# One row buffer instead of two for the second expert layer of a two-layer decoder kernel

## What is computed

```python
pos = jnp.sum(jnp.cumsum(oh, axis=0) * oh, axis=-1) - 1      # place of a token in its expert
valid = pos < CAP                                             # CAP = 192
xb = jnp.zeros((E, CAP + 1, H), x.dtype).at[flat_e, pos_c].set(x[tok])   # E = 48 experts
gu = jnp.einsum('ech,eoh->eco', xb, gate_up_proj)
g, u = jnp.split(gu, 2, axis=-1)
out = jnp.einsum('eci,ehi->ech', silu(g) * u, down_proj)
final = jnp.zeros_like(x).at[tok].add(y * w[:, None])         # 8 experts of a token summed
...
x = layernorm(x + final)
```

## Time and profile before

| | us |
|---|---|
| median of 3 runs | 2174.53 |
| lowest, highest run | 2170.31, 2190.89 |
| span of the profiled execution | 2197.3 |
| of it, first to last even scatter issue in `kept_experts` | 1798.09 to 2151.90 |
| of it, first load issue of `finish` to the end | 2158.30 to 2197.3 |

### The profile page before, as it was taken

The page is one execution under the profiler, slowest core; times in us unless marked ns, Lnnn a source line. Parts: engine busy times, 40 slices in busy tenths (PEclk is TensorE's granted clock), DMA queues, the critical chain, the costliest instruction groups (busy, mean ns, idle before and its releaser), DMA issues. The chain is left out here.

```text
span 2197.3 us, 34584 instructions
## 1 busy us (share of the span) xinstructions
PE 1743.9 (79%) x9155; PEld 1385.2 (63%) x9156; DVE 1522.4 (69%) x2887; ACT 959.1 (44%) x1867; POOL 1110.5 (51%) x806
## 2 busy tenths in 40 slices
PE   4899889247999999999999798687841159999990
PEld 4566565126888888888888455464521158888880
DVE  5466776664777787777887323978879657777774
ACT  4355362221444444434444323535333147777773
POOL 1000624553677777777687200025447647777761
PEclk9898999666999999999999898888875579999995
DMA  6011011024777787888887511021010269999867
GB/s 262 1 39 58 20 58 39 1 78 150 202 201 191 197 233 201 209 211 216 205 244 163 189 44 38 23 74 58 1 58 1 91 205 260 258 254 255 255 156 251
DMA packets 134248, 310.14 MB, mean 141 GB/s; under 512 B 30632, under 2 KB 31240, under 8 KB 132520
## 3 DMA queue, kind: packets, MB, share of 16 engines
q1 hardware_dynamic: 68728, 196.24, 25.7%
q0 software_dynamic: 63168, 108.89, 24.6%
q10 hardware_dynamic: 2288, 4.29, 0.5%
HBM read 234.48 MB, written 93.16 MB: 149 GB/s over the span
## 5 line engine op out<-in xcount | busy, mean ns | idle before, releaser
L98 POOL DMA_INDIRECT tab_rows<-pair,slot x256 | 312.6, 1221 | 487.0 <-DVEq L751 314.6
L1253 POOL DMA_INDIRECT xg<-x_rows,ids x167 | 211.3, 1265 | 65.6 <-issue 42.6
L90 PE MATMUL gu<-wgu_h,xgT_h 128*128 x648 | 234.5, 362 | 6.9 <-DVE xgT_l L1429 4.1
L90 PE MATMUL gu<-wgu_l,xgT_h 128*128 x648 | 220.2, 340 | 0.0
L90 PE MATMUL gu<-wgu_h,xgT_l 128*128 x648 | 219.1, 338 | 0.0
L1262 POOL DMA_INDIRECT odd_rows<-ysb,ids x80 | 149.0, 1862 | 76.0 <-DMA odd_rows<-ysb,ids 41.5
L1262 POOL DMA_INDIRECT acc_rows<-ysb,ids x80 | 141.6, 1769 | 67.6 <-DMA acc_rows<-ysb,ids 33.1
L1309 ACT ACTIVATE ysb<-yp,wts 128x512 f32<-128x512 f32 x160 | 110.2, 688 | 144.0 <-PE yp L1536 112.3
L90 PE MATMUL guk<-xgT_hk,wgu_hk 128*128 128x192 f32 x576 | 161.2, 280 | 0.0
L1429 DVE TENSOR_TENSOR xgT_l<-tpx,xgT_h 128x512 fp32r<-128x512 f32 x163 | 112.3, 689 | 68.5 <-ACT xgT_h L1295 62.9
L1299 ACT ACTIVATE sg<-gu 128x192 f32<-128x192 f32 x162 | 53.6, 331 | 240.2 <-PE gu L90 214.8
(11 more groups left out here) (498 smaller groups left out, 5067.8 us busy)
## 6 DMA issues: line engine op xcount, KB each, us to landing
wgu_sb<-in_wgu SPq DMA_DIRECT2D x64, 768.0 KB
wgu_sbk<-in_wgu SPq DMA_DIRECT2D x48, 768.0 KB
wd_sb<-in_wd SPq DMA_DIRECT2D x64, 256.0 KB
wd_sbk<-in_wd SPq DMA_DIRECT2D x48, 256.0 KB
ct<-in_ctxT SPq DMA_DIRECT2D x8, 1024.0 KB
wd_sb<-in_wd SPq DMA_DIRECT2D x64, 128.0 KB
wd_sbk<-in_wd SPq DMA_DIRECT2D x48, 128.0 KB
odd_rows<-zero SPq DMA_DIRECT2D x1, 4352.0 KB, 15.3
```

The lines of the kernel that those rows point to most:

```text
L90: i = nc.tensor.matmul(out, left(k), right(k), start=(start and k == 0 and m == 0), stop=(k == ops - 1 and m == 2))
L98: nc.gpsimd.indirect_dma_start(out=tab, out_offset=bass.IndirectOffsetOnAxis(ap=s["slot"][:, n:n + 1].bitcast(U32), axis=0), in_=s["pair"] ...
L1253: nc.gpsimd.indirect_dma_start(out=xg[:, t % G, :], out_offset=None, in_=x, in_offset=bass.IndirectOffsetOnAxis(ap=ids[:, t:t + 1].bitcast ...
```

## The change

Both tiles of an expert are now added into `acc1`. Tile t with t of 2 or more waits for both tiles of the preceding expert. For an even tile, those are t-2 and t-1. For an odd tile, they are t-3 and t-2, for which the even tile ahead of it has already waited. `odd1` is gone, and so are its clear in `mixer_two` and its eight loads and sixteen adds in `finish`. The counts of the semaphores follow. The order of the instructions on each engine is unchanged.

```diff
 def kept_experts(nc, d, s):
 
-    tab, x, acc = d["tab1"], d["x5"], (d["acc1"], d["odd1"])
+    tab, x, acc = d["tab1"], d["x5"], d["acc1"]
...
             def scatter_add(t):
                 if t >= 2:
-                    pool.wait_ge(s_add[t % 2], (t // 2) * 16)
+                    for n in range(2):
+                        pool.wait_ge(s_add[n], (t // 2) * 16)
                 pool.wait_ge(s_ye, t + 3)
                 nc.gpsimd.indirect_dma_start(
-                    out=acc[t % 2], out_offset=bass.IndirectOffsetOnAxis(ap=ids[0:rows(t), t:t + 1].bitcast(U32), axis=0),
+                    out=acc, out_offset=bass.IndirectOffsetOnAxis(ap=ids[0:rows(t), t:t + 1].bitcast(U32), axis=0),
...
             for n in ("x5", "acc1"):
                 sp.dma_start(d[n][TOK:TOK + P, :], zero[:, :]).then_inc(s_zero, 16)
-            clear_rows(sp, d["odd1"], zero, s_zero)
...
-            sp.wait_ge(s_zero, 128)
+            sp.wait_ge(s_zero, 112)
...
-        BASE, FIRST, LATER = B * 20, 3 * GT, 2
+        BASE, FIRST, LATER = B * 20, 2 * GT, 2
...
             for n in range(NG):
-                for t, dst in ((d["acc1"], xb), (d["odd1"], xbo)):
-                    sp.dma_start(dst[:, n, :, :], rows(t, n)).then_inc(loaded[n][0], 16)
+                sp.dma_start(xb[:, n, :, :], rows(d["acc1"], n)).then_inc(loaded[n][0], 16)
...
             for n in range(NG):
                 sem_n, there = loaded[n]
-                dve.wait_ge(sem_n, there + 32)
-                for j in range(GT):
-                    c.done(nc.vector.tensor_tensor(xb[:, n, j, :], xb[:, n, j, :], xbo[:, n, j, :], ALU.add))
-                c.wait()
+                dve.wait_ge(sem_n, there + 16)
```

More of the change, by code:

```diff
@@ L2071, in _ @@
                 settle(pool, passed)
-                pool.wait_ge(s_zero, 128)
+                pool.wait_ge(s_zero, 112)
                 scatter(nc, d["tab1"], s, E1 * REG1 - 1, s_scat)
@@ L2220, in step @@
                 if b is None:
-                    act.wait_ge(s_zero, 128)
+                    act.wait_ge(s_zero, 112)
                 averaged(a)
@@ L2767, in finish @@
         xb = sb("xb5", [P, NG, GT, D])
-        xbo = sb("xbo5", [P, NG, GT, D])
         xo = sb("xo5", [P, NG, GT, D])
@@ L2778, in finish @@
         loaded = [(s["mixer"][0], 2 * B * 16 + 16), (s["mixer"][1], 2 * B * 16), (s["weights"][0], NI * 16), (s["weights"][1], NW * 16),
-                  (s["mixer"][7], 128), (s["router"][0], 2 * ROUTED), (s["router"][1], 2 * ROUTED), (s["router"][4], 2 * ROUTED)]
+                  (s["mixer"][7], 112), (s["router"][0], 2 * ROUTED), (s["router"][1], 2 * ROUTED), (s["router"][4], 2 * ROUTED)]
         passed = s["passed"]
@@ L2911, in build @@
     for n, rows, cols, dt in (("x2", TOK + P, D, F32), ("x5", TOK + P, D, F32), ("acc0", TOK + P, D, F32), ("acc1", TOK + P, D, F32),
-                              ("odd0", TOK + P, D, F32), ("odd1", TOK + P, D, F32),
+                              ("odd0", TOK + P, D, F32),
                               ("tab0", E0 * REG0 + P, 2, I32), ("tab1", E1 * REG1 + P, 2, I32)):
```

## The result

| | before | changed |
|---|---|---|
| median of 4 runs, us | 2178.56 | 2236.54 |
| lowest to highest run | 2170.31 to 2190.89 | 2224.46 to 2241.88 |
| span of the profiled execution | 2197.3 | 2222.7 |

The ratio is 1.0251 with a 95% interval of 1.021 to 1.0292: the changed kernel is 2.5% slower, about 55 us. The forecast was +26.4 us, 1.2%, with a range up to 2224. The direction was right. The size was half of what came, and the median lies outside the range.

A forecast was written before the change was run, and what follows sets the result against it. ACT, DVE and PE were taken to pace the kernel, with POOL's closed chain taking over after the change. +36.1 + 1.7 - 11.4 = +26.4 us on the median gave 2200.9 us, 1.2% slower, range 2182 to 2224.

The forecast's parts named there:

- What bounds the kernel: Steady part of the second experts: ACT, DVE and PE set the pace, 7.67 us an expert; add into HBM hidden.
- The closed chain: POOL, second experts: even issue, gather, odd issue, odd landing, wake-up, next even issue; period 8.51 us, +36.1 us.
- sign of being wrong: Wrong if the steady period stays under 8.1 us or passes 9 us, or last stage returns under 8 us.
- L: POOL's time from odd scatter start to the start its landing permits: 5.3 us; above 4.45 us experts pay.
- the bound by packets: POOL's queue q0 in the kernel before: odd scatter landed 3.8 to 4.7 us after start, so L 4.7 to 5.6 us.
- The fixed phase: POOL against DVE: ACT and DVE follow the odd landing, phase much like today's, so the 2.22 us odd issue stays.
- collides with the expert weights: Rival, second experts: odd tile shares engines with weights; period 10.2 us, time 2282, about 2235 at half; chance 0.08.
- The last experts: Last four intervals, without gathers: each takes 6.40 us, 25.6 us against 23.94, +1.7 us.
- Who is behind the wait: Gathers queued behind POOL's wait run ten tiles ahead; ACT stops for `ysbk` first, so PE's transposes do not starve.
- The last stage: Half the loads and 16 DVE adds go; ACT paces groups at 2.24 us; -11.4 us, bounds 8 to 13.
- The clear: Clear of 4352 KB, 14.8 us: nobody listed as waiting for POOL's loads behind it, counted as 0.
- The clock: Rival: granted clock falls as PE idles; at 0.87 no cost, at 0.75 +52 us more; chance 0.03.

The follow-up runs named there:

- buffer_by_expert: Kernel before with both tiles of an expert in one buffer, the next expert's in the other, waits two experts back: 0.9972 times before.
- the two wait experiments: Kernel before, each scatter waiting for both preceding-expert tiles: 1.0284 times before. Changed kernel, odd scatter also waiting for its even tile: 2415.56 us beside 2200.72 of before.
- clear_put_back: Changed kernel with the clear of the second buffer restored in the second mixer: median 2235.3 against 2236.54 us.
- loads_behind_landing: Changed kernel with weight loads from the ninth expert on requested only after an odd tile has landed: 1.0166 times before, period 8.80 us.
- scatters_side_by_side: Changed kernel with both scatters of an expert issued back to back and both gathers behind them: 1.0023 times before, period 8.22 us.
- side_by_side_loads_behind: Changed kernel with both scatters back to back and weight loads requested behind the odd landing: 1.0066 times before, period 8.38 us.
- side_by_side_loads_behind_even: Changed kernel with both scatters back to back and weight loads requested when an even tile has landed: 1.0051 times before, period 8.29 us.
- odd_waits_for_even: Changed kernel with the odd scatter also waiting for its own expert's even tile: 2415.56 us beside 2200.72 of before, period 12.36 us.
- short_subtractions: Changed kernel with DVE's weight subtractions cut to 4 columns for all but the first experts: period 8.58 us, +29 us.
- loads_behind_short_subtractions: Changed kernel with subtractions cut to 4 columns and weight loads held until the odd tile has landed: period 8.54 us, +33 us.
- half_loads_short_subtractions: Changed kernel with subtractions cut and weight loads cut to half their columns behind the fourth expert: period 8.15 us, +14 us.
- hardly_any_weights: Changed kernel with weight loads of all experts but the first four cut to 4 columns: period 8.29 us, +0.4 us.
- no_weights_short_subtractions: Changed kernel with both weight loads and DVE's weight subtractions cut to 4 columns in later experts: period 8.12 us, +2 us.
- loads_behind_even_short: Changed kernel with subtractions cut and weight loads requested when an even tile has landed: period 8.32 us, +35 us.
- loads_behind_even: Changed kernel, whole, with weight loads requested when an even tile has landed: period 8.89 us, +19 us.

## Why the prediction fell short

**What bounds the kernel** held. In before and in buffer_by_expert the other engines pace the stage at 7.67 us, and the landing is hidden only because a tile looks back two scatters or more.

**The closed chain** held, 43 times of 43, and by the two wait experiments. The wake-up was 0.87 us against 0.89 from the rows. The prediction's own sign of being wrong came too: the period passed 9 us.

**L was mis-sized**, and this is the step that failed. The forecast took 4.54 us from the last odd scatter of the stage and corrected it for the longer issue only, though it said itself that this scatter had no load traffic beside it. The two halves of L were wrong in opposite ways. The issue was 1.69 us on average instead of 2.22, because the phase moved. The landing with wake-up was 4.04 us instead of 3.12, partly because of the loads. Together L was 5.74 instead of 5.3 us. The even leg took 3.35 instead of 3.21 us, since some even issues were now the held ones (mean 1.67 us instead of 1.57). That makes 43 x (0.44 + 0.14) = 25 us.

The 3.12 us was too small in both of its parts. That last odd scatter landed 4.07 us after its start by the landing marks, and the next stage's load was issued 0.47 us later. So the sum held 2.65 us of landing, where the changed kernel shows 3.17, and 0.47 us of wake-up, where POOL takes 0.87. The second part could be seen beforehand, since the bound by packets already used 0.89 us.

"No row of before shows this L" was true of the rows, but not of the trace. The odd landing has its marks in the kernel before as well: in the 39 of 43 experts with all sixteen on record, it came 4.64 us after the start of the scatter. With the wake-up L is 5.5 us and the sum about +35 us. That is nearer, and still 18 us short of the 52.7 us between the profiles: 10 for L at 5.74, 6 for the even leg and 2 for the last experts.

**The fixed phase** was the wrong sentence behind it: "the two keep a fixed phase again, much like today's". The odd issues vary from 1.45 to 3.02 us and the gaps from 4.5 to 9.6 us. The kernel of before has one phase: the subtractions hold the odd issue, and the loads are requested within 0.1 us of its end in nearly every expert. The landing is then mostly 2.2 to 2.6 us behind the issue, and the changed kernel has that phase in 8 of 43 experts only. Late landings in before (four of 43 were 3.7 us or more behind the issue by their marks, of which the waits view shows three) entered only through a rival. They showed what a collision costs. The rival "collides with the expert weights" had this mechanism and came closest, at a chance of only 0.08. That its 2235 us fits so well is partly luck. It is the price for half of the experts, and 15 of 43 collided. Its own two ends, 2200.9 with none and 2282 with all, give 2241 at half and 2229 at 15 of 43. (The lower end of the forecast's range is off by 2 us in the same way: L = 4.9 gives 2184, not 2182.)

**Adding up the pieces.** For the other kernels with the changed last stage, the same sum is 43 x (period - 7.67) plus the change of the last four intervals and -12.2 us. Beside it stands the measured ratio turned into us, and for kernels with one run its difference to the median of before.

| kernel | sum, us | measured, us |
|---|---|---|
| clear_put_back | +65 | +53 |
| loads_behind_landing | +41 | +37 |
| scatters_side_by_side | +16 | +5 |
| side_by_side_loads_behind | +22 | +15 |
| side_by_side_loads_behind_even | +18 | +11 |
| odd_waits_for_even (one run) | +207 | +215 |
| short_subtractions (one run) | +31 | +29 |
| loads_behind_short_subtractions (one run) | +28 | +33 |
| half_loads_short_subtractions (one run) | +12 | +14 |
| hardly_any_weights (one run) | +18 | +0.4 |
| no_weights_short_subtractions (one run) | +11 | +2 |
| loads_behind_even_short (one run) | +20 | +35 |
| loads_behind_even (one run) | +44 | +19 |

Most agree within 12 us. Three of the single runs miss by 15 to 25 us, in both directions. Runs of before in one set lie up to 29 us apart, so a single run can't test the sum more closely. The periods come from the stage itself. Their own spread of up to 0.3 us makes 13 us over 43 intervals.

**The last experts** took 6.95 us each instead of 6.40: issue and landing 4.24 us, wake-up 0.82 and 1.89 from even to odd. The forecast had 4.54 us for issue, landing and wake-up together, from the one scatter with 4.07 + 0.47 us. Most of the difference is the wake-up again.

**Who is behind the wait.** "PE's transposes do not starve" was wrong. PE waited 52 us for gathers, and ACT only 6 us for a place in `ysbk`: POOL's lag reaches the others through the gathers queued behind the scatter. It cost nothing by itself, since `ysbk` was always ready before the landing.

**The last stage** gave 12.2 us against 11.4. ACT's pace there was 2.07 us a group, not 2.24. **The clear** was rightly at 0. **The clock** was granted at 0.93 and did not become the bound, as its rival's arithmetic had it.

## What to carry to other kernels

A wait on the transfer issued just before turns a hidden landing into the period of its queue. Let the wait look back as many transfers as the landing lasts. That takes enough buffers that nothing nearer can touch the same rows, so count issue, landing and wake-up before merging two buffers into one. Do not size such a landing from the kernel in which it is hidden or from the stage's quiet end: there it has a phase that the change can shift. Look whether the trace has its landing marks. Price it with the other queue's traffic beside it, and give the collision case the chance that its share of the time suggests. Here that share is large: an expert has 1152 KB of weights, and 0.95 MB took 53.8% of 4.4 us behind the second odd scatter shown, so I estimate 3 of every 8 to 9 us.

## What the runs showed of the hardware

- A scatter issue on GpSimd of 1.47 us becomes up to 3.02 us when DVE subtracts operands in SBUF beside it, and it ends with DVE's chain (1878.96 against 1878.94, and within 0.03 us in all 8 cases). With the subtractions cut, none of 76 issues was over 1.74 us.
- The wake-up from a transfer's last landing mark to the start of the waiting GpSimd issue was 0.86 to 0.87 us in 42 of 43 cases, and 0.82 us in the last four intervals.
- An accumulating scatter of 64 rows landed 2.4 us behind its issue without load traffic. With 250 KB or more beside it, the mean was 4.1 us in the changed kernel. The amount alone does not tell: in the kernel before, with the loads requested 0.06 us behind the issue's end, most landings with 200 to 300 KB beside them were 2.2 to 2.4 us behind it.
- The median of the kernel before was 2172 to 2210 us, depending on the set of runs. Only comparisons within one set were used.
